# Two Mamba-2 layers in an AdaLN block on one Trainium2 core: parts of a tile's work moved on four engines, and the loop's back edge written another way

## The reference

```python
mod = (silu(c) @ wmod).reshape(8, 6, 1, 512)
sa, ca, ga, sb, cb, gb = ...                       # ga, gb kept away from zero
h = layernorm(x) * (1 + ca) + sa
for i in range(2):                                 # two Mamba-2 layers
    u = layernorm(h, ln_w[i], ln_b[i])
    z, xBC, dt = split(u @ in_w[i].T)              # 1024 + (1024 + 64 + 64) + 16 columns
    dt = softplus(dt + dt_bias[i])
    xBC = silu(conv4(xBC) + conv_b[i])             # depthwise, 4 taps along time
    xh, B, C = split(xBC)                          # 16 heads of 64
    state_t = exp(dt_t * A) * state_{t-1} + (dt_t * x_t) B_t ;  y_t = state_t C_t
    y = (y + D * xh) * silu(z)
    y = y * rsqrt(mean(y * y) + eps) * rms_w[i]
    h = h + y @ out_w[i].T
x = x + ga * h
x = x + gb * channel_mix(layernorm(x) * (1 + cb) + sb)
```

## Time and profile before

| | us |
|---|---|
| median of 3 runs (4337.45 to 4342.61) | 4339.32 |
| the profiled execution | 4342.61 |
| its span, first to last instruction | 4340.8 |
| TensorE busy (share of the span) | 4017.9 (93%) |
| VectorE busy | 3475.0 (80%) |
| ScalarE busy | 2908.6 (67%) |
| POOL busy | 2027.6 (47%) |
| mean granted TensorE clock | 0.961 |

### The profile page before, as it was taken

The page is one execution under the profiler, slowest core; times in us unless marked ns, Lnnn a source line. Parts: engine busy times, 40 slices in busy tenths (PEclk is TensorE's granted clock), DMA queues, the critical chain, the costliest instruction groups (busy, mean ns, idle before and its releaser), DMA issues. The chain is left out here.

```text
span 4340.8 us, 100166 instructions
## 1 busy us (share of the span) xinstructions
PE 4017.9 (93%) x38872; PEld 3611.2 (83%) x38872; DVE 3475.0 (80%) x5217; ACT 2908.6 (67%) x4904; POOL 2027.6 (47%) x1572
## 2 busy tenths in 40 slices
PE   4499999999999999958999999999999995799989
PEld 1399989898989899958999999999999994677777
DVE  8588888888888888867888888888888885576664
ACT  4577767676767677746777777777777773666655
POOL 7344444444444444423444444444444444556664
PEclk6699999999999999979999999999999997899999
DMA  8300000000000000020000000000100002122220
GB/s 326 136 31 31 31 31 31 31 31 31 30 31 30 31 31 31 26 97 26 31 31 31 31 33 30 31 31 34 39 31 30 31 26 96 71 93 93 91 74 35
DMA packets 108579, 220.18 MB, mean 51 GB/s; under 512 B 10760, under 2 KB 11272, under 8 KB 107272
## 3 DMA queue, kind: packets, MB, share of 16 engines
q1 hardware_dynamic: 108176, 214.25, 13.8%
HBM read 146.97 MB, written 67.24 MB: 49 GB/s over the span
## 5 line engine op out<-in xcount | busy, mean ns | idle before, releaser
L503 PE MATMUL l_ring<-l_u_hi,l_wi_lo 128*128 128x256 f32 x4608 | 1318.9, 286 | 43.1 <-DVE l_u_lo L933 29.0
L503 PE MATMUL l_ring<-l_u_lo,l_wi_hi 128*128 128x256 f32 x4608 | 1297.5, 282 | 0.0
L503 PE MATMUL l_ring<-l_u_hi,l_wi_hi 128*128 128x256 f32 x4608 | 1296.8, 281 | 0.0
L985 DVE SCALAR_TENSOR_TENSOR l_xc<-l_raw,l_prm,l_xc 128x256 f32<-128x256 f32 x1536 | 952.8, 664 | 115.1 <-ACT l_xc L761 96.9
L503 PEld LDWEIGHTS l_ring<-l_u_hi,l_wi_lo 128*128 128x128 f32 x4608 | 874.5, 190 | 67.9 <-issue 29.8
L503 PEld LDWEIGHTS l_ring<-l_u_lo,l_wi_hi 128*128 128x128 f32 x4608 | 874.8, 190 | 12.9 <-issue 1.3
L503 PEld LDWEIGHTS l_ring<-l_u_hi,l_wi_hi 128*128 128x128 f32 x4608 | 874.8, 190 | 0.0
L1169 POOL TENSOR_TENSOR l_g<-l_g 128x512 f32<-128x512 f32 (+2 forms) x384 | 355.4, 926 | 1096.8 <-ACT l_g L822 1076.7
L1140 POOL TENSOR_TENSOR l_rhs<-l_cum,l_small 32x1024 fp32r<-32x1024 f32 x256 | 497.1, 1950 | 214.5 <-PE l_wide L565 145.2
L1160 POOL TENSOR_TENSOR l_g<-l_g,l_zs 128x1024 f32<-128x1024 f32 x128 | 305.8, 2389 | 452.2 <-DVE l_g L1032 450.6
L503 PE MATMUL l_ring<-l_wo_hi,l_g_lo 128*128 128x512 f32 x1024 | 414.1, 404 | 18.9 <-DVE l_g_lo L1037 11.5
(11 more groups left out here) (175 smaller groups left out, 8104.1 us busy)
## 6 DMA issues: line engine op xcount, KB each, us to landing
l_hn<-h_scratch SPq DMA_DIRECT2D x64, 512.0 KB, 3.8
l_res<-h_scratch SPq DMA_DIRECT2D x128, 256.0 KB, 3.6
h_scratch<-l_res SPq DMA_DIRECT2D x128, 256.0 KB, 2.1
m_rows<-in_x SPq DMA_DIRECT2D x16, 1024.0 KB, 9.4
h_scratch<-m_rows SPq DMA_DIRECT2D x16, 1024.0 KB, 7.3
f_x<-in_x SPq DMA_DIRECT2D x16, 1024.0 KB, 7.0
f_h<-h_scratch SPq DMA_DIRECT2D x16, 1024.0 KB, 8.9
out<-f_x SPq DMA_DIRECT2D x64, 256.0 KB, 2.0
```

The source lines that it names most:

```text
L503: last = nc.tensor.matmul(out, a, c, start=(k == 0), stop=(k == n - 1))
L985: ins = nc.vector.scalar_tensor_tensor(out=acc, in0=raw[:, (s + c) % 2, k, tap:tap + TB], scalar=prm_sb[:, w:w + 1], in1=acc, op0=ALU.mult ...
```

## The change

Four things are changed, all in `mamba_layer`. The loop is now `eng.Fori(...)`, which is the same loop without the hint. TensorE does `square_sum(b, s, 0)` behind `states(1,1)` and `outputs(1,1)`. VectorE does `row_stats(nxt2)` and `sum_parts(nxt)` earlier, behind `taps(nxt, 0)`. POOL does `inv_std(nxt2)` ahead of `skip_term(1)`, and `moving(nxt, 0)` ahead of `squares(0)`. No instruction but the hints is removed, none is added, and no wait is changed.

```diff
-            with nc.Fori(b0 + first, b0 + nseq - 1, engines=[eng.engine], hint_back_edge=True) as b:
+            with eng.Fori(b0 + first, b0 + nseq - 1) as b:
...
                 out_product(b, s, 0, bank(s, USE_O[0]))
-                square_sum(b, s, 0)
                 states(b, s, 1, 1)
                 outputs(b, s, 1, 1)
+                square_sum(b, s, 0)
...
                     taps(*nxt, 0)
+                if n2:
+                    row_stats(*nxt2)
+                if n1:
+                    sum_parts(*nxt)
                 y_read(b, s, 0, 1)
                 x_read(b, s, 1)
                 matrices(b, s, 1, 0)
                 low_g(b, s, 0)
-                if n2:
-                    row_stats(*nxt2)
-                if n1:
-                    sum_parts(*nxt)
+                if n1:
                     taps(*nxt, 1)
...
                 moving(b, s, 3)
+                if n2:
+                    inv_std(*nxt2)
                 skip_term(b, s, 1)
                 gate(b, s, 0)
+                if n1:
+                    moving(*nxt, 0)
                 squares(b, s, 0)
-                if n2:
-                    inv_std(*nxt2)
-                if n1:
-                    moving(*nxt, 0)
+                if n1:
                     moving(*nxt, 1)
```

More of the change, by code:

```diff
@@ L1181, in body @@
                 moving(b, s, 3)
+                if n2:
+                    inv_std(*nxt2)
                 skip_term(b, s, 1)
                 gate(b, s, 0)
-                squares(b, s, 0)
-                if n2:
-                    inv_std(*nxt2)
                 if n1:
                     moving(*nxt, 0)
+                squares(b, s, 0)
+                if n1:
                     moving(*nxt, 1)
```

## The result

The changed kernel takes 4467.16 us (median of 4 runs, 4464.31 to 4470.78), the kernel before 4338.39 beside it: a ratio of 1.0301, 95% interval 1.0281 to 1.0320. The prediction was 4461 with a range of 4420 to 4480.

What follows compares the result with a forecast made beforehand. TensorE was taken to bound both layers. 60 tiles x 1.49 us = 89 us, plus 32 for the hint, made 121 on the profiled 4342.6, so 4464; with the runs' median 3.3 lower, 4461, range 4420 to 4480.

Steps and rivals of the forecast that it cites:

- The stall at `exponents(1,1)`: TensorE waits for `x_read(1)`, delayed by `row_stats` and `sum_parts` moved ahead on VectorE: a new stall of 1.35 us per tile.
- The walk along the rows: Following VectorE's profile rows up to `exponents(1,1)`: of the 2.51 us moved ahead, 1.35 us reach TensorE as a stall.
- The term of `square_sum`: `square_sum` behind `outputs(1,1)` delays VectorE's `mean_square` and the unbroken row behind it, so `out_product(1)` waits 0.33 us more per tile.
- The give-back at the next `exponents(0,1)`: TensorE's wait there in the next tile goes, since its chain starts from `proj(8)`, ahead of the stall: 0.19 us back.
- POOL and L941: POOL's reordering costs nothing; L941 on VectorE gets 1.35 us shorter, but that ends in idling for ScalarE: counted as nothing.
- The hint: Without it, layer 1's six taken back edges on TensorE cost what layer 0's do: 5.4 us each, 32 us.
- Layer 0 pays although hinted: Layer 0's back edges on TensorE are already long with the hint, so removing it changes nothing there.
- VectorE's refetch: VectorE may stall at unhinted edges too, beside TensorE's standstill of 3.5 us: counted as nothing, at most 5 x 1 us.
- (a): Rival: the hint is worth nothing on TensorE in layer 1, 4428 us; chance 0.11.
- (b): Rival: the VectorE shift is absorbed by the shorter L941 or unseen slack, 4379 us; chance 0.06.
- (c): Rival: the new stalls pull TensorE's clock down, half a microsecond or more per tile on top, 4500 us; chance 0.05.
- (d): Rival: not slower, VectorE's early work pays and both late waits go; 4311 us or 4343; chance 0.04.

Runs made afterwards that it cites:

- slot 192: The kernel before with TensorE's loops of both layers begun at place 192 of a 16 KB code block, hints kept: 4366.50 us, ratio 1.0055.
- slot 0: The kernel before with TensorE's loops of both layers begun at place 0 of a 16 KB code block, hints kept: 4317.40 us, ratio 0.9940.
- slot 40: The kernel before with TensorE's two loops begun at place 40 of a 16 KB code block, nothing else changed: 4313.96 us, ratio 0.9943.

## Why the prediction was right

**The stall at `exponents(1,1)`: right.** Predicted 1.35 us, measured 1.34. The walk along the rows gave a slack of 1.16, the changed kernel shows 2.51 - 1.34 = 1.17; with VectorE's steps alone or one of them it is 1.27 to 1.33, and with all steps moved and the hint kept 1.22 to 1.24. So that the two figures agree to 0.01 is in part luck: 0.07 of the stall goes when the hint comes back (third to fourth pair 4.58 us), and 0.03 more belongs to the other moved steps. Neither was followed up.

**The term of `square_sum`: the path right, the size a little off.** `out_product(1)` moved back by 0.27 us (predicted 0.33). It starts 0.15 behind the end of `low_g(1)` in both kernels, with TensorE idle ahead of it (0.11 us before, 0.17 now), so the delay does arrive over VectorE. Counted from `out_product(0)`, `mean_square` starts at 8.12 instead of 7.68 us, which is 0.44 later, but `y_read(1,1)` behind it at 8.20 instead of 7.93. The row behind `mean_square` was not unbroken, as the prediction took it to be: in the kernel before VectorE was idle there for 0.10 us, until `outputs(1,1)` was done.

```profile
2493.51 0.69 DVE L1032 TENSOR_TENSOR l_g<-l_g,l_ps_y 128x512 f32<-128x512 f32 x1
```

What the prediction did not see is that TensorE's own row grew beside this, by 0.21 us. From the start of `out_product(0)` to the block behind it are 5.69 us instead of 5.59, `square_sum` takes 0.24 instead of 0.21, and the matmuls of `proj(6)` to `proj(8)` and what stands behind them 0.08 more. `square_sum` alone shows the same growth.

**The give-back at the next `exponents(0,1)`: mis-sized.** Predicted 0.19, measured 0.06. The chain to `x_read(0)` starts from `proj(8)`, and I took that to be ahead of the delay; with TensorE's row 0.21 longer, `proj(8)` is late by 0.21 of the 0.27 as well, and only the other 0.06 come back. In both kernels VectorE's next taps wait 1.2 us for ScalarE (L761), whose input is `proj(8)`.

**POOL and L941: right**, shown by undoing POOL's order alone (third to fourth pair 4.60 us with the new order, 4.58 with the old). In the tile above VectorE idles 0.71 us for L591 and 0.47 for L810 with the time that L941 saved.

**The hint: right in size, incomplete on layer 0.** 5.5 us an edge in layer 1 (predicted 5.4), between 5.1 with the hint alone removed and 5.9 with it put back. "Layer 0 pays although hinted" held for the profile, not for every run: the kernel before spreads over 4325 to 4348 us, about four edges of 5.4. Since most of its edges are long in most runs, the sum hardly noticed. VectorE's refetch, costed at nothing, exists in both layers and costs nothing.

**The rivals.** (a) fell with the run of the hint alone, (b) with L941 relieved and the tile no shorter for it. (c) did not occur: the clock was granted in full in the loops away from the edges, in spite of 1 us of idling in each tile. (d) needed a slack of 2.51 us; there are 1.2 to 1.3.

**The sum.** 93 and 33 against 89 and 32: the forecast was 6 us low. Its range was written a little wider than its terms give: 1.2 to 1.6 us a tile and 30 to 39 for the edges make 4441 to 4474.

What stays open: why the packet goes out ahead of some hinted branches and not of others in the same execution, why TensorE's row grows with `square_sum` in its new place, and what else moves single runs by some 9 us.

## What to carry to other kernels

Work moved ahead of something that the bounding engine waits for is free up to the slack there and costs one for one behind it, so measure the slack as the start of the waiting step less the end of what it waits for, plus idling ahead of that. A tuned loop whose body is fetched anew in every iteration (here 19 to 20 packets) can have a price per iteration that neither its instructions nor its waits show: read the closing branch's duration at every edge, and where hinted edges are long, try the loop at another place in its code block. Compare variants by the period of the repeated stretch in the profile before trusting medians, when something unrelated to the edit varies by as much as the effect.

## What the runs showed of the hardware

- Whether a hinted back edge is short depends on where the loop lies: at slot 192 none of 11 edges was short, at slot 0 ten were, at slot 40 all, with the same instructions. A long edge costs 5.4 us, 3.1 of them in the branch (3.5 against 0.45 us), the rest at half clock behind it.
- One execution can serve some edges of a loop and not others: 458 to 493 ns and over 3500 ns in one layer. With the hint the two kinds differ without exception in one thing: a 16 KB packet of instructions goes out ahead of the branch (100 short edges) or does not (32 long ones).
- VectorE, with a loop body about a tenth of TensorE's in instructions (466 against some 4670 in an iteration, weight loads counted), also stands still at unhinted edges (2.8 us), and with the hint never did in these traces.
- A tiny matmul's place matters: two matmuls with one column (L606) moved behind `outputs(1,1)` lengthened TensorE's own row by 0.21 us a tile, with no wait to show for it.
